# Splitting the softmax subtraction 208 to 176 columns between VectorE and GpSimd, instead of 160 to 224

## The reference, cut to what matters

```python
w_attn = softmax(einsum('ncq,nck->nqk', q, k * scale), axis=2)
a      = einsum('nqk,nck->ncq', w_attn, v)
out    = einsum('oc,bchw->bohw', proj_w, a) + proj_b + x
```

## Time and profile before

| | |
|---|---|
| median of 3 runs | 4401.74 us (4397.77 to 4403.0) |
| the profiled execution | 4398.31 us |
| its span, first to last instruction | 4396.5 us |
| TensorE, VectorE, ScalarE, GpSimd busy | 94%, 78%, 63%, 41% of the span |
| mean granted TensorE clock | 0.99 of full speed |

### The profile page before, as it was taken

The page is one execution under the profiler, slowest core; times in us unless marked ns, Lnnn a source line. Parts: engine busy times, 40 slices in busy tenths (PEclk is TensorE's granted clock), DMA queues, the critical chain, the costliest instruction groups (busy, mean ns, idle before and its releaser), DMA issues. The chain is left out here.

```text
span 4396.5 us, 84946 instructions
## 1 busy us (share of the span) xinstructions
PE 4117.0 (94%) x29976; PEld 2458.3 (56%) x29976; DVE 3426.9 (78%) x3564; ACT 2790.3 (63%) x2981; POOL 1802.6 (41%) x584
## 2 busy tenths in 40 slices
PE   7998899999999999998999979999999999999989
PEld 4554555555555555554555545555555555555545
DVE  4222899999999999998433339999999999999972
ACT  1111788888888888886001027888888888888840
POOL 0000455555555555555100005555555555555540
PEclk9999999999999999999999999999999999999999
DMA  4334111212112111120444441212112111111216
GB/s 191 136 127 142 31 49 39 61 35 55 43 49 51 38 50 44 47 68 32 157 144 162 139 133 24 61 35 59 38 50 55 38 48 39 52 41 50 61 43 208
DMA packets 234733, 321.67 MB, mean 73 GB/s; under 512 B 12081, under 2 KB 221105, under 8 KB 233649
## 3 DMA queue, kind: packets, MB, share of 16 engines
q1 hardware_dynamic: 214512, 292.54, 23.0%
q10 hardware_dynamic: 20160, 28.32, 1.8%
HBM read 188.69 MB, written 132.12 MB: 73 GB/s over the span
## 5 line engine op out<-in xcount | busy, mean ns | idle before, releaser
L617 POOL TENSOR_TENSOR prob<-prob,mx 128x1344 f32<-128x1344 f32 x576 | 1781.6, 3093 | 2433.0 <-DVE two_tiles L894 1445.0
L772 ACT ACTIVATE prob<-psum_att 128x1152 f32<-128x1152 f32 x1152 | 1290.4, 1133 | 597.6 <-DVE run L874 336.4
L706 PE MATMUL psum_att<-qst,kst 128*128 128x384 f32 x6912 | 1420.2, 349 | 48.7 <-DMA kst<-qk_scratch 27.9
L785 ACT ACTIVATE prob<-prob 128x1152 f32<-128x1152 f32 x1152 | 1299.2, 1166 | 37.5 <-POOL prob L617 37.5
L706 PEld LDWEIGHTS psum_att<-qst,kst 128*128 128x128 f32 x6912 | 1177.1, 190 | 185.6 <-ACT prob L772 91.4
L719 PE MATMUL psum_att<-prob,vst 128*32 128x384 f32 x13824 | 1237.5, 491 | 34.6 <-ACT pvr L791 29.3
L617 DVE TENSOR_TENSOR prob<-prob,mx 128x960 f32<-128x960 f32 x576 | 974.1, 1691 | 173.0 <-ACT mx L779 173.0
L874 DVE TENSOR_TENSOR run<-psum_att,run 128x1152 f32<-128x1152 f32 x768 | 1004.3, 1347 | 13.0 <-PE psum_att L706 12.8
L719 PEld LDWEIGHTS psum_att<-prob,vst 128*32 128x32 f32 x13824 | 399.5, 109 | 625.1 <-issue 594.7
L894 DVE TENSOR_TENSOR two_tiles<-prob 128x768 f32<-128x768 f32 x576 | 565.9, 983 | 0.0
L314 PE MATMUL psum<-xc_l,wq 128*128 128x384 f32 x1536 | 504.3, 490 | 11.0 <-DVE hl_l L419 5.8
(11 more groups left out here) (59 smaller groups left out, 1906.7 us busy)
## 6 DMA issues: line engine op xcount, KB each, us to landing
qk_scratch<-hl_l SPq DMA_DIRECT2D x48, 1536.0 KB, 5.6
qst<-qk_scratch SPq DMA_DIRECT2D x192, 384.0 KB, 5.6
kst<-qk_scratch SPq DMA_DIRECT2D x192, 192.0 KB, 3.3
v_scratch<-vo_l SPq DMA_DIRECT2D x24, 768.0 KB, 3.5
vst<-v_scratch SPq DMA_DIRECT2D x96, 192.0 KB, 2.5
att_scratch<-ob ACTq DMA_DIRECT2D x96, 192.0 KB, 1.9
attc_l<-att_scratch SPq DMA_DIRECT2D x24, 768.0 KB, 5.5
x_sb<-in_x SPq DMA_DIRECT2D x8, 1152.0 KB, 14.1
```

The lines of the kernel that those rows point to most:

```text
L617: return engine.tensor_tensor(x, x, m, ALU.subtract)
L706: mm = nc.tensor.matmul(psum[:, 3 * e + k, 0:CH], kst[:, e, (3 * c + k) * P:(3 * c + k + 1) * P], qst[par][:, 2 * w + e, :], start=(w == 0 ...
L772: nc.scalar.activation(chunk_of(par, c, e), s_bank(e), ACT.Copy).then_inc(copied, 1)
L785: nc.scalar.activation(x, x, ACT.Exp, scale=SCALE).then_inc(exp_done, 1)
```

## The change

One constant changes. VectorE's part of each subtraction grows from 160 to 208 columns of 384, which is 960 to 1248 elements per partition in an instruction. GpSimd's falls from 224 to 176 columns, 1344 to 1056 elements. No instruction is added or removed, and no wait or order changes.

```diff
-SHIFT_DVE = 160
+SHIFT_DVE = 208
```

## The result

The changed kernel takes 4374.48 us (median of 4 runs, 4371.94 to 4375.56), the kernel before 4401.42 us beside it. The ratio is 0.9939 with a 95% interval of 0.9922 to 0.9956: 27 us or 0.6% faster. The forecast was 4363 us, so about two thirds of the gain came. The profiled execution took 4374.46 us against 4398.31 us, 24 us less.

What follows compares the result with a forecast made beforehand. VectorE was taken to bound the attention stages. 94 blocks at -0.36 us (-33.8) and the tail (-4.6) took 4398.31 to 4359.9 us profiled, 4363 us for the median; range 4350 to 4394 us.

Steps and rivals of the forecast that it cites:

- VectorE sets the pace: In the attention stages VectorE is full but for one wait per block, while TensorE has 1.69 us per block in hand.
- The stall lasts to the end of GpSimd's instruction: VectorE instructions with both operands in SBUF make no progress until GpSimd's ends; VectorE loses 3.69 us per block.
- +0.30 us for VectorE's longer part: Each of six subtractions per block gets 288 more elements at 1.04 ns, 0.30 us each, +1.80 us on the path.
- GpSimd's part 2.45 us: GpSimd's subtraction part of 1056 elements takes 2.45 us, 0.63 us less, so stalls give back 2.16 us per block.
- A line through the two unlike forms: Rival: GpSimd's instruction is mostly fixed cost, 2.80 us for 1056 elements; +0.59 us per block, 4457 us, chance 0.12.
- TensorE's spare time: Between TensorE's waits at 1032.09 and 1048.59, VectorE's path shortens 0.63 us; TensorE can give 0.69 us, sufficing by 0.06.
- TensorE becomes the bound: Rival: at the fold and scores of c = 5 TensorE's chain takes back half; -0.18 us per block, 4380 us, chance 0.12.
- the likeliest case alone: The forecast without its rivals, for the whole kernel: 4354 to 4373 us, chance 0.66.
- The tail: VectorE's and GpSimd's parts alternate strictly; -0.33 us for each of 7 steps in each of 2 layers, -4.6 us.
- The forecast's own sum: Per block, 1.80 us for VectorE's longer parts minus 2.16 us of stalls given back: -0.36 us.
- the other direction: VectorE's longer part could also hold GpSimd up, but not where GpSimd starts under the maxima; no size given.

Runs made afterwards that it cites:

- the fit: The changed kernel with VectorE's columns set per step, (184, 168, 208, 208, 208, 84), instead of 208 throughout: 4298.8 us, ratio 0.9770 to the kernel before.
- the early copy: ScalarE's copy of the weighted sums moved ahead of the exponential for e = 1 of c = 3; on the fit, 4292.9 us, 0.9753 of the kernel before.

## Why the prediction was right, point by point

- *VectorE sets the pace:* right, and enough for the sign. The block's length follows VectorE's own instructions, plus the gaps in front of the maxima of c = 5 and, once the subtraction of c = 0 ends early enough, of c = 1.
- *The stall lasts to the end of GpSimd's instruction:* right. At c = 0 after the change GpSimd ends at 1051.16 and the longer subtraction at 1052.47 us, 1.31 us later, where 1.02 + 0.30 was the estimate. The runs with 192 columns show a partial stall of the size that GpSimd's length leaves.
- *+0.30 us for VectorE's longer part:* measured 0.30.
- *GpSimd's part 2.45 us:* measured 2.475. A line through the two unlike forms, the rival of the other side, is refuted: at 960, 1056, 1152 and 1344 elements the medians are 2.256, 2.475, 2.673 and 3.081 us. The Trainium skill's 2.6 cycles per element at 1.2 GHz, 2.17 ns (GPSIMD Engine Reference, "Elementwise — side-by-side cycle accounting"), agrees with the measured 2.10 ns to 3%. The 0.025 us that the estimate missed cost 0.03 us per block at c = 0.
- *TensorE's spare time:* this is the step that was mis-sized. I gave TensorE 0.06 us of margin at the fold and some 0.3 us at the second maximum of c = 5, and looked at the end of the second half of the scores. The first maximum needs only the first half, and there the margin was zero. Between c = 3 and 5 VectorE's own path became shorter by 0.10 us (+0.18 - 0.28), and all of it went to the new gap of 0.11 us. That is 94 x 0.11 = 10 us of the missing 14 us between the forecast of -38 and the profiled -24 us; GpSimd's length gives 94 x 0.03 = 3 us more. The rival "TensorE becomes the bound" was thus half true: it named the engine and the place, and guessed 0.18 us for what is 0.11. The measured 4374.5 us lies nearer to its 4380 than to the forecast's 4363, and just above the 4354 to 4373 given for the likeliest case alone; the stated range holds it because this rival was taken in.
- *The tail:* right. Two parts of GpSimd there are 4.72 us apart (2029.81 and 2034.53 us), 0.31 less than in the earlier trace rows; 0.33 was forecast. Not all steps of the tail follow that pattern, as the prediction had it: the last four parts start 4.78 to 4.80 us apart before and 4.49 or 4.50 after, 0.3 us less as well. From its first reductions to the end of GpSimd's last part a tail became 2.9 us shorter (38.3 to 35.4 us), where 2.3 was forecast.

What was neither in the forecast nor in its rivals: 208 is past the best even split. The forecast's own sum would have said so. With 192 columns it is 6 x 0.20 - (0.25 + 0.12 + 3 x 0.42) = -0.43 us against -0.36 with 208, for most of the stalls at c = 2, 3 and 4 and in the fold are gone by then, and 16 columns more cost 0.60 us and give back 0.53. I computed only the one point that the change offers. The sum would have had the order of the two right but not the size: measured, the blocks are 0.18 us apart on average (33.33 and 33.51 us), 0.07 from the sum and 0.11 from the gap, which with 192 columns is paid back in the fold.

Left open: what the hold in front of the maxima of c = 1 would give if it were moved. With the fit it is 0.30 us per block, 28 us in 94, with the early copy or without, and no run moves it. TensorE is busy 1425.67 of 1450 us with the fit, which leaves it about 0.5 us per block, so not much more than that hold is left to gain on this path.

## What to carry to other kernels

When two engines share operands' access so that one stalls behind the other, a split is judged by where each part of the other engine ends, instruction by instruction; one constant for stretches with different room leaves stalls in one and idle room in another, and the fit of each step brought nearly four times what the change did (102 and 27 us). Before counting on a shorter instruction, follow the signal that it sends through the other engines to the next thing that the same engine waits for: if that loop is already tight, only what lies ahead of it counts. A margin is to be read at the first instruction that needs the data, not at the last.

## What the runs showed of the hardware that was not expected

The exclusion works in both directions, as the Trainium skill's rule has it (SBUF — State Buffer, "SBUF: two separate sides"). The prediction named the other direction and ruled it out where GpSimd starts under the maxima. The trace shows it where I had not looked for it, in the tail of the changed kernel, where VectorE's subtraction starts first:

```profile
2039.07 1.45 DVE L617 TENSOR_TENSOR prob<-prob,mx 128x1248 f32<-128x1248 f32 x1
```

```profile
2034.53 2.43 POOL L617 TENSOR_TENSOR prob<-prob,mx 128x1056 f32<-128x1056 f32 x1 [2.26 <-DVE two_tiles L894]
2039.22 3.60 POOL L617 TENSOR_TENSOR prob<-prob,mx 128x1056 f32<-128x1056 f32 x1 [2.26 <-DVE two_tiles L894]
```

GpSimd's instruction takes 3.60 us instead of 2.43, and VectorE's is not lengthened. The kernel before has it too, 3.89 us (from 2050.14 us) instead of 3.06. And a GpSimd part of 1800 elements, which runs under two maxima and a wait of VectorE, took 4.07 us and left VectorE's wait at 1.66 to 1.76 us, no longer than before.
